# Two layers of recurrent mixing, routed experts and attention on one Trainium2 core: the choice of tokens moved into the layer 0 mixer and expert block

## The chip, the cores and the metric

The kernel runs on one core of one Trainium2 chip. The metric is the device time of one execution in microseconds. Three runs of the kernel before gave 1783.84, 1784.66 and 1787.1 us, so the median is 1784.66 us. TensorE does the matrix products and transposes, VectorE and ScalarE the elementwise work, GpSimd small elementwise work and indirect DMAs, and SyncE only issues DMAs.

## The reference, cut to what matters

Eight sequences of 512 tokens with 256 features each pass through two layers. This change touches layer 0 only. Its mixer and its experts both read the normalised input `xn`:

```python
qkv = rms_norm(xn) @ w_qkv.T;  q, k, v = split(qkv);  q, k = rms_norm(q), rms_norm(k)
w = exp(k);  y = sigmoid(q) * cumsum(w * v) / (cumsum(w) + 1e-6)      # along the sequence
u, g = split(y @ w_swiglu.T);  s = xn + (u * silu(g)) @ w_out.T       # the mixer

probs = softmax over the 512 tokens of (silu(xn @ router_w1) @ router_w2).T   # 16 experts a sequence
weights, tokens = top_k(probs, 64);  weights /= weights.sum() + 1e-9          # the choice of tokens
out_e = (silu(x_e @ w1[e]) * (x_e @ w2[e])) @ w3[e]                           # x_e: the chosen rows
f = scatter-add of weights * out_e;   x = x + s * silu(f)
```

Each of the 16 experts picks 64 of the 512 tokens of every sequence. So there are 8 x 16 = 128 lists, one for each partition. Layer 1 (attention with 16 heads, then 8 experts of which each token takes 2) follows and is not changed.

## The kernel before

The kernel is written engine by engine in blocks; all engines meet at the end of a block. Layer 0 has three of them.

`layer0_norm` normalises `xn`, keeps its transpose in `m.xnT`, and computes the router's logits. Its SyncE queue ends with eight 512 KB stores of zeros into `f`, the tensor to which the experts add (line 220).

`choose_tokens` (lines 108 to 184) is a block of its own. TensorE turns the logits so that each of the 128 partitions has one list of 512 (line 131). ScalarE takes the exponentials (L140). VectorE then runs eight rounds, each of which takes the eight largest values (L160), finds their places (L162) and strikes them out (L163). It scales the shares, adds the first row of the sequence to the places (L166 to L175), TensorE turns both tables back (L134, L135), and VectorE copies them to `k.slot_row` and `k.slot_share` (L182).

`layer0_mix_and_experts` does the rest. A product of the experts and of the mixer's gates is made of three products of `float32r` halves (`product3`, L93): each operand is split into a high part, copied by ScalarE, and a low part, subtracted by VectorE (`high_w` and `low_w` for the weights, `high_x` and `low_x` for the rows). The raw weights arrive in three tiles `raw[0..2]`. The swiglu weights of the mixer, `wsw`, come first and share `raw[0]` with `w1`.

Two lists set the order of every engine's work. `expert` has six entries for each expert: four `up` (a quarter of the hidden features each, both products) and two `down`. `mixing` has twelve for each sequence: four `qkv` (products of a tile of 128 tokens), four `sum` (the running sums, by products with a triangle and with ones; VectorE divides, L694 to L703), one `turn` (transposes of `y`), two `gates` and one `out`. `order` is made once and each engine walks through it: the first four `qkv`, then four `up` of expert 0, and from there one entry of `expert` and one of `mixing` by turns:

```python
order, LEAD = mixing[:T] + expert[:FC], FC
for i in range(len(expert) - LEAD):
    order += [expert[LEAD + i]] + mixing[T + i:T + i + 1]
order += mixing[T + len(expert) - LEAD:]
```

Some steps hang on others. `exps(n)` on ScalarE (exponentials of keys and of queries of sequence n) and `partial(n)` on GpSimd (sums of tiles, L634, L636) and `keys_values(n)` on VectorE (L686) come with the first `down` of expert 2n. `factors(n)` on GpSimd (L613 to L627) needs the squares of all four `qkv` of sequence n. `fetch(e)` on GpSimd gathers the 512 rows of expert e with four indirect DMAs (L644), `combine(e)` adds its results to `f` (L651), and the block ends when the last of these has landed. VectorE's queue begins with the low parts of `wsw`, `w1`, `w2` and `w3` (L746, L728), then comes the first copy of a qkv tile (L678, L679).

## Time and profile before

| | us |
|---|---|
| median of three runs | 1784.66 (1783.84 to 1787.1) |
| the profiled execution, its own time | 1782.32 |
| its span, first to last instruction | 1780.6 |
| the block that chooses tokens, TensorE's first to VectorE's last instruction | 51.12 to 74.37 |
| first product of the mixer | 75.06 |
| first product of expert 0 | 107.81 |
| last product of expert 15 | 617 |
| first load of layer 1 issued | 631.86 |

Over the whole span TensorE is busy 1573.8 us (88%), VectorE 1171.3 us (66%), ScalarE 922.1 us (52%) and GpSimd 729.9 us (41%). Such shares are means over stages with different limits, and the rows further down show the stage that the change touches. Times in the profile count from the first instruction. TensorE's granted clock is given as a share of its full speed, 1.00 being 2.4 GHz and 0.50 being 1.2 GHz. A matrix record overlaps the next one a little, so a busy time can exceed the time that passes.

### The profile page before, as it was taken

Reading aid. Unit: us, or ns where it says so; the run is one execution under the profiler, and the core shown is the slowest. Engines: PE = TensorE matmul, PEld = TensorE weight load, DVE = VectorE, ACT = ScalarE, POOL = GpSimd, SP = SyncE. Lnnn points to the kernel's source line nnn. Section 1 sums busy time; section 2 is a strip of 40 time slices with the busy share of each in tenths; the row PEclk is TensorE's granted clock in tenths of the full one; section 3 lists DMA queues with packets and bytes.
Section 4 is the critical chain, followed back from the end, with each engine's and each line's share of the span. In section 5 each row is a group of like instructions: output and inputs, shape, how many; then the busy total and the mean of one; then the engine's idle time right before and its main releaser. Section 6 shows DMA issues by size and latency. Waiting matters only on the chain.

```text
span 1780.6 us, 27053 instructions
## 1 busy us (share of the span) xinstructions
PE 1573.8 (88%) x9562; PEld 1141.8 (64%) x9562; DVE 1171.3 (66%) x1851; ACT 922.1 (52%) x1428; POOL 729.9 (41%) x661
## 2 busy tenths in 40 slices
PE   6269999999999829963899999999999999999975
PEld 4147787777777716641677777777777777777631
DVE  6536756756765536647666666777777777777647
ACT  2134554454454322310455556767776767676645
POOL 4213533443353254412233323455555555555410
PEclk9689999999999958985899999999999999999976
DMA  6423644644433167953334244666666666767464
GB/s 228 165 83 95 150 111 100 173 89 114 106 74 104 16 191 267 323 196 113 106 99 122 94 137 127 187 165 180 171 179 177 178 179 170 187 165 192 109 186 152
DMA packets 218919, 265.39 MB, mean 149 GB/s; under 512 B 19616, under 2 KB 160416, under 8 KB 218784
## 3 DMA queue, kind: packets, MB, share of 16 engines
q1 hardware_dynamic: 191904, 227.92, 42.2%
q0 software_dynamic: 26880, 35.73, 11.2%
q8 instruction: 77, 1.26, 0.3%
q14 instruction: 58, 0.48, 0.1%
HBM read 174.30 MB, written 88.75 MB: 148 GB/s over the span
## 4 chain that ended last, share of the span: by engine, by line
PE 38%; SPq 4%; DVE 4%; DMA 2%; ACT 1%; issue 1%; POOL 0%; DVEq 0%; ACTq 0%
PE a_hidden_bank L93 15%; PE a_bank L93 8%; PE a_bank L1519 5%; PE a_max_bank L1488 5%; PE a_score_bank L1509 3%; DMA a_ka<-qk 2%; SPq L1311 2%; SPq L1315 1%; PE a_max_bank L1534 1%; DVE a_neg_max L1784 1%; PE a_bank L1526 1%; DVE a_w20lo L1825 1%; ACT a_xThi L1667 1%; DVE a_hT1lo L1815 0%; SPq L1377 0%
## 5 line engine op out<-in xcount | busy, mean ns | idle before, releaser
L1645 ACT ACTIVATE a_prob<-a_score_bank 128x1024 f32<-128x1024 f32 x240 | 246.2, 1026 | 254.5 <-PE a_score_bank L1509 218.7
L1784 DVE TENSOR_REDUCE a_neg_max<-a_max_bank 128x2 f32<-128x1024 f32 x249 | 304.1, 1221 | 90.7 <-PE a_max_bank L1488 90.4
L1441 POOL DMA_INDIRECT fs<-a_y,a_token x80 | 127.1, 1589 | 188.9 <-ACT a_y L1693 165.1
L1488 PE MATMUL a_max_bank<-a_ka,a_qa 48*128 48x512 f32 x498 | 127.7, 509 | 23.2 <-DVE a_neg_max L1784 13.1
L1519 PE MATMUL a_bank<-a_prob,a_va 128*32 128x512 f32 x1024 | 145.8, 643 | 0.8 <-ACT a_prob L1645 0.6
L1807 DVE SCALAR_TENSOR_TENSOR a_tg<-a_tg,a_hidden_bank 128x512 f32<-128x512 f32 x112 | 76.8, 686 | 83.2 <-ACT a_tg L1655 83.2
L651 POOL DMA_INDIRECT f<-e_ye,c_slot_row x64 | 100.9, 1577 | 74.2 <-issue 50.5
L1509 PE MATMUL a_score_bank<-a_qa,a_ka 50*128 50x512 f32 x480 | 100.7, 415 | 5.4 <-DMA a_qa<-a_ml 3.0
L425 PE MATMUL e_bank<-m_wqkv,x_rows 128*128 128x512 f32 (+1 forms) x256 | 92.4, 506 | 14.7 <-DVE e_qkv L679 13.3
L739 DVE TENSOR_TENSOR e_h<-e_bank,e_sge 128x512 f32<-128x512 f32 x64 | 44.3, 692 | 85.8 <-ACT e_sge L563 85.3
L1488 PEld LDWEIGHTS a_max_bank<-a_ka,a_qa 48*128 48x128 f32 x498 | 47.9, 189 | 70.0 <-DVE a_neg_max L1784 27.6
L93 PE MATMUL a_hidden_bank<-a_xThi,a_w31hi 128*128 128x256 f32 x288 | 89.8, 312 | 0.0
L1655 ACT ACTIVATE a_tg<-a_hidden_bank 128x512 f32<-128x512 f32 x112 | 67.2, 600 | 41.9 <-PE a_hidden_bank L93 41.4
L644 POOL DMA_INDIRECT e_xg<-xn,c_slot_row x64 | 70.8, 1106 | 43.7 <-issue 43.7
L93 PE MATMUL e_bank<-e_w3hi,e_heThi 128*128 128x256 f32 x256 | 81.1, 317 | 7.8 <-DVE e_heTlo L743 7.8
L1811 DVE TENSOR_TENSOR a_h<-a_hidden_bank,a_tg 128x512 f32<-128x512 f32 x112 | 77.5, 692 | 13.0 <-PE a_hidden_bank L93 1.2
L93 PE MATMUL a_hidden_bank<-a_xThi,a_w11hi 128*128 128x256 f32 x288 | 85.0, 295 | 0.0
L93 PE MATMUL a_hidden_bank<-a_xThi,a_w31lo 128*128 128x256 f32 x288 | 82.5, 287 | 0.0
L93 PE MATMUL a_hidden_bank<-a_xTlo,a_w31hi 128*128 128x256 f32 x288 | 82.5, 286 | 0.0
L425 PEld LDWEIGHTS e_bank<-m_wqkv,x_rows 128*128 128x128 f32 x256 | 49.0, 197 | 52.1 <-issue 34.5
L93 PE MATMUL a_hidden_bank<-a_xTlo,a_w11hi 128*128 128x256 f32 x288 | 81.9, 284 | 0.0
L93 PE MATMUL a_hidden_bank<-a_xThi,a_w11lo 128*128 128x256 f32 x288 | 81.7, 284 | 0.0
(350 smaller groups left out, 4772.9 us busy)
## 6 DMA issues: line engine op xcount, KB each, us to landing
a_raw<-in_W SPq DMA_DIRECT2D x120, 512.0 KB, 4.9
e_raw<-in_w SPq DMA_DIRECT2D x48, 512.0 KB, 4.4
a_qa<-qk SPq DMA_DIRECT2D x192, 64.0 KB, 3.7
a_ka<-qk SPq DMA_DIRECT2D x192, 64.0 KB, 3.2
xs<-c_pad SPq DMA_DIRECT2D x20, 516.0 KB, 8.5
a_xg<-xs SPq DMA_DIRECT2D x20, 516.0 KB, 4.7
qk<-p_hi SPq DMA_DIRECT2D x32, 256.0 KB, 5.7
qk<-p_lo SPq DMA_DIRECT2D x32, 256.0 KB, 5.5
```

Source lines behind the costliest of these rows:

```text
L93: ins = nc.tensor.matmul(out, a[i][x], b[l][y], start=first and n == m == 0, stop=last and n == len(pairs) - 1 and m == 2)
L425: ins = nc.tensor.matmul(bank[:, 0:f1 - f0], m.xnT[:, n, ch, t * P:(t + 1) * P], m.wqkv[:, ch, f0:f1], start=ch == 0, stop=ch == DC - 1)
L644: nc.gpsimd.indirect_dma_start(xg[u][:, t, :], None, xn_rows, bass.IndirectOffsetOnAxis(k.slot_row[:, e, t:t + 1], 0)).then_inc(xg_in[u], 16)
L651: nc.gpsimd.indirect_dma_start(f_rows, bass.IndirectOffsetOnAxis(k.slot_row[:, e, t:t + 1], 0), ye[:, t, :], None, compute_op=ALU.add).the ...
L1441: nc.gpsimd.indirect_dma_start(f_rows, bass.IndirectOffsetOnAxis(token[x % 4][:, t:t + 1], 0), y[:, t, :], None, compute_op=ALU.add).then_ ...
L1488: nc.tensor.matmul(max_bank(g, m)[:, s, :], qa[q][rows, p, t * P:(t + 1) * P], ka[q][rows, p, :], start=True, stop=True).then_inc(p1_ps, 1)
L1509: nc.tensor.matmul(score_bank(g, u)[:, s, :], ka[q][rows, p, j * P:(j + 1) * P], qa[q][rows, p, :], start=True, stop=True).then_inc(s_ps, 1)
L1519: ins = nc.tensor.matmul(OB[rows, :], va[g % NR][:, j, rows], prob[j % 2][:, h_, :], start=j == 0, stop=j == T - 1, tile_position=(0, 32 * ...
L1645: nc.scalar.activation(prob[j % 2][:, 2 * p:2 * p + 2, :], score_bank(g, u)[:], ACT.Exp, scale=float(D) ** -0.5).then_inc(p_done, 1)
L1784: nc.vector.tensor_reduce(neg_max[:, g % 2, :, T * p + t], max_bank(g, m)[:], AX.X, ALU.max, negate=True).then_inc(mx_done, 1)
L1807: nc.vector.scalar_tensor_tensor(tg[:], tg[:], 1.0, GATE[:], ALU.add, ALU.mult).then_inc(act_done, 1)
L1811: nc.vector.tensor_tensor(h[:], VALUE[:], tg[:], ALU.mult).then_inc(h_done, 1)
```

## The change

The block `choose_tokens` is gone. Its steps stand at the beginning of `layer0_mix_and_experts`, before the walk through `order`, and its two score tiles and the tile of exponentials lie in `sge` and `h`, which the experts use later. The banks of `GATE` and `YE` hold its transposes.

- **VectorE** runs the eight rounds first, and after rounds 0, 2, 4 and 6 copies one qkv tile of sequence 0.
- **TensorE** turns the logits, does the four `qkv` of sequence 0 beside the rounds, turns the two tables, and then does four `sum` of sequence 0 and two `qkv` of sequence 1 before expert 0. The walk starts at `FIRST = 10` instead of 4 in `mixing`, so each sequence's steps lie beside the expert before, and the six entries of expert 15 have no mixer step after them.
- **GpSimd** makes the low parts of `wsw` and of the first weights in VectorE's place, then `factors(0)`, `fetch(0)`, `partial(0)` and `fetch(1)`.
- **ScalarE** alternates high parts with squares, and takes `exps(0)` before expert 0.
- **SyncE** loads `wsw` into `raw[2]` instead of `raw[0]`, so `w1` and `w2` need no wait and `w3` waits for the low part of `wsw`.

```diff
-def choose_tokens(nc, R, k):
...
+    prob, ex = [sge[:, i, :] for i in range(2)], h[:, 0, :]
...
+    LISTED, SLOTS = 2, 6
+    wsw_raw = raw[2][:].rearrange("p (c f) d -> p c (f d)", c=DC)
...
-    order, LEAD = mixing[:T] + expert[:FC], FC
+    FIRST = T + 6
+    order, LEAD = expert[:FC], FC
     for i in range(len(expert) - LEAD):
-        order += [expert[LEAD + i]] + mixing[T + i:T + i + 1]
-    order += mixing[T + len(expert) - LEAD:]
+        order += [expert[LEAD + i]] + mixing[FIRST + i:FIRST + i + 1]
...
-                elif i == 0:
-                    sp.wait_ge(yT_lo, 1)
+                elif i == 2:
+                    sp.wait_ge(wsw_lo, 1)
...
-            sp.dma_start(raw[0][:], wsw_d).then_inc(raw_in[0], 16)
-            for i in (1, 2, 0):
+            sp.dma_start(wsw_raw, wsw_d).then_inc(raw_in[2], 16)
+            for i in range(3):
                 load(i, 0)
...
+            for t in range(T):
+                ins = nc.tensor.transpose(GATE[:, t * P:(t + 1) * P], k.logits[:, t].rearrange("p b e -> p (b e)"), k.ident[:])
+            ins.then_inc(choice_ps, 1)
             pe.wait_ge(m.w_in, 2 * 16)
+            for t in range(T):
+                qkv_(0, t)
+            pe.wait_ge(choice_done, LISTED)
+            nc.tensor.transpose(YE[0][:, 0:P], rows[:].rearrange("p a c -> p (a c)"), k.ident[:])
+            nc.tensor.transpose(YE[1][:, 0:P], share[:].rearrange("p a c -> p (a c)"), k.ident[:]).then_inc(choice_ps, 1)
+            for t in range(T):
+                sum_(0, t)
+            qkv_(1, 0)
+            transpose_x(0)
+            qkv_(1, 1)
...
+            act.wait_ge(choice_done, 1)
+            nc.scalar.activation(ex, GATE[:], ACT.Exp, bias=neg_max[:], accum_out=total[:]).then_inc(choice_exp, 1)
+            act.wait_ge(raw_in[2], 16)
+            nc.scalar.activation(wsw[0][:], wsw_raw, ACT.Copy).then_inc(yT_hi, 1)
+            squared(0, 0)
             for i in range(3):
                 high_w(i, 0)
+                squared(0, i + 1)
+            exps(0)
+            squared(1, 0)
+            high_x(0)
+            squared(1, 1)
...
-                    if i == 0 and a % 2 == 0:
-                        exps(a // 2)
+                    if i == 0 and a % 2 and a + 1 < E0:
+                        exps((a + 1) // 2)
...
+            pool.wait_ge(yT_hi, 1)
+            nc.gpsimd.tensor_tensor(wsw[1][:], wsw_raw, wsw[0][:].bitcast(F32), ALU.subtract).then_inc(wsw_lo, 1)
+            for i in range(3):
+                low_w(i)
+            factors(0)
+            pool.wait_ge(choice_done, SLOTS)
             fetch(0)
+            partial(0)
             fetch(1)
...
-            dve.wait_ge(yT_hi, 1)
-            nc.vector.tensor_tensor(wsw[1][:], raw[0][:], wsw[0][:].bitcast(F32), ALU.subtract).then_inc(yT_lo, 1)
-            for i in range(3):
-                low_w(i, 0)
...
+            for r in range(CAP // 8):
+                eight, src, dst = best[:, 8 * r:8 * r + 8], prob[r % 2], prob[(r + 1) % 2]
+                own.step(nc.vector.max(eight, src))
+                own.wait()
+                own.step(nc.vector.max_index(place[:, 8 * r:8 * r + 8], eight, src))
+                own.step(nc.vector.match_replace(dst, eight, src, -1.0))
+                own.wait()
+                if r % 2 == 0:
+                    copy_qkv(0, r // 2)
...
+            keys_values(0)
+            for t in range(T):
+                divide(0, t)
+            copy_qkv(1, 0)
+            low_x(0)
+            copy_qkv(1, 1)
```

On VectorE, the end of the choice before the change and what stood behind it:

```order
L182 COPY c_slot_share<-ct_bank 64x64
L182 CAST c_slot_row<-ct_bank 64x64
L182 COPY c_slot_share<-ct_bank 64x64
L122 UNCONDITIONAL_BRANCH
L670 UNCONDITIONAL_BRANCH
L746 TENSOR_TENSOR e_wswlo<-e_raw,e_wswhi 128x1024
L728 TENSOR_TENSOR e_w10lo<-e_raw,e_w10hi 128x1024
L728 TENSOR_TENSOR e_w20lo<-e_raw,e_w20hi 128x1024
L728 TENSOR_TENSOR e_w3lo<-e_raw,e_w3hi 128x1024
L678 COPY e_qkv<-e_bank 128x512
L679 COPY e_qkv<-e_bank 128x256
```

The four low parts stand ahead of the first qkv copy here.

After the change the last two rounds read as follows, with the copy of the fourth qkv tile (L641 and L642 are the lines of L678 and L679) between them:

```order
L721 MAX e_best<-e_sge 128x8
L723 MAX_INDEX e_place<-e_best,e_sge 128x8
L724 MATCH_REPLACE e_sge<-e_best,e_sge 128x512
L641 COPY e_qkv<-e_bank 128x512
L642 COPY e_qkv<-e_bank 128x256
L721 MAX e_best<-e_sge 128x8
L723 MAX_INDEX e_place<-e_best,e_sge 128x8
L724 MATCH_REPLACE e_sge<-e_best,e_sge 128x512
```

The four subtractions of weights have left this queue, and the qkv copies now stand between the rounds.

On TensorE, the choice and the first tile's products before (the last row of the first fence is followed by three more such pairs, then by the transposes of the gathered rows):

```order
L131 MATMUL ct_bank<-c_ident,c_logits 128x128 x4
L134 MATMUL ct_bank<-c_ident,ct_rows 128x128
L135 MATMUL ct_bank<-c_ident,ct_share 128x128
L122 UNCONDITIONAL_BRANCH
L419 UNCONDITIONAL_BRANCH
L425 MATMUL e_bank<-m_wqkv,x_rows 128x512 x2
L425 MATMUL e_bank<-m_wqkv,x_rows 128x256 x2
```

All products of the mixer stand behind both tables' transposes here.

And the changed queue behind the fourth tile's products, from the two tables' transposes (L434, L435) to those of the gathered rows (L403) and the products behind them:

```order
L434 MATMUL e_bank<-c_ident,e_rows 128x128
L435 MATMUL e_bank<-c_ident,e_share 128x128
L369 MATMUL e_bank<-e_wkv,c_upper 128x512 x2
L372 MATMUL e_bank<-e_wkv,c_ones 128x512
L369 MATMUL e_bank<-e_wkv,c_upper 128x512
L372 MATMUL e_bank<-e_sums,c_ones 128x512
L369 MATMUL e_bank<-e_wkv,c_upper 128x512
L372 MATMUL e_bank<-e_sums,c_ones 128x512
L358 MATMUL e_bank<-m_wqkv,x_rows 128x512 x2
L358 MATMUL e_bank<-m_wqkv,x_rows 128x256 x2
L403 MATMUL e_bank<-c_ident,e_xg 128x128 x8
L358 MATMUL e_bank<-m_wqkv,x_rows 128x512 x2
```

The running sums (L369, L372) and the products of sequence 1 now lie ahead of the transposes of expert 0's rows.

On GpSimd the changed kernel's block begins with the four low parts, and the gathers of expert 0 stand behind the factors of sequence 0; before, the eight gathers came first:

```order
L611 TENSOR_TENSOR e_wswlo<-e_raw,e_wswhi 128x1024
L608 TENSOR_TENSOR e_w10lo<-e_raw,e_w10hi 128x1024
L608 TENSOR_TENSOR e_w20lo<-e_raw,e_w20hi 128x1024
L608 TENSOR_TENSOR e_w3lo<-e_raw,e_w3hi 128x1024
L564 TENSOR_SCALAR e_small<-e_ssq 128x8
L567 TENSOR_TENSOR e_small<-e_small,m_r2sq 128x4 x2
L571 TENSOR_SCALAR e_small<-e_small 128x8
L573 TENSOR_TENSOR e_small<-e_small,m_half 128x8
L577 TENSOR_TENSOR e_scale<-e_small,m_r2neg 128x4
L578 TENSOR_TENSOR e_scale<-e_small,m_r 128x4
L595 DMA e_xg<-xn,c_slot_row 128x256 x4
L585 TENSOR_TENSOR e_sums<-e_wkv 128x512
```

The gathers (L595) moved behind six small steps and four large ones, and the partial sums (L585, L587) moved between the two experts' gathers.

## Rows read from the trace of the kernel before

**Rows 1.** Windows: from:to, length, busy us (records) per engine, TensorE clock, DMA share, GB/s
```profile
50.00:55.00 5.00, 0.84 (x6) 0.53 (x6) 2.80 (x9) 2.06 (x3) 0.13 (x1) 0.88 1.00 333
...
133.00:587.40 454.40, 441.44 (x2147) 341.57 (x2146) 291.88 (x426) 229.67 (x455) 191.81 (x176) 1.00 0.45 109
...
587.40:617.00 29.60, 27.42 (x138) 21.53 (x137) 18.18 (x26) 9.92 (x16) 6.26 (x4) 1.00 0.17 18
```

**Rows 2.** Timeline, the block that chooses: start us, duration, engine, line, operation, tiles
```profile
51.12 0.63 PE L131 MATMUL ct_bank<-c_ident,c_logits 128*128 128x128 f32 x4 [0.90 <-PEq L200]
...
54.04 0.69 DVE L160 MAX8 ct_best<-ct_prob 128x8 f32<-128x512 f32 x1
...
71.47 0.22 DVE L166 TENSOR_REDUCE ct_wsum<-ct_best 128x1 f32<-128x64 f32 x1
...
74.15 0.22 DVE L182 COPY c_slot_share<-ct_bank 64x64 f32<-64x64 f32 x1
```

**Rows 3.** Timeline, opening of the mixer and expert block
```profile
75.06 5.46 PE L425 MATMUL e_bank<-m_wqkv,x_rows 128*128 128x512 f32 x8 [1.47 <-PEq L122]
...
79.06 1.06 ACT L580 ACTIVATE e_wswhi<-e_raw 128x1024 fp32r<-128x1024 f32 x1 [25.78 <-DMA e_raw<-in_w_swiglu]
...
85.86 1.06 ACT L552 ACTIVATE e_w10hi<-e_raw 128x1024 fp32r<-128x1024 f32 x1 [5.74 <-DMA e_raw<-in_w]
...
90.47 0.69 DVE L678 COPY e_qkv<-e_bank 128x512 f32<-128x512 f32 x1
...
91.08 0.41 DVE L679 COPY e_qkv<-e_bank 128x256 f32<-128x256 f32 x1
```

**Rows 4.** Timeline, from the last opening copy to the first expert product, and GpSimd's factors
```profile
105.00 0.42 ACT L522 ACTIVATE e_squares<-e_qkv 128x256 f32<-128x256 f32 x1 [3.06 <-DVE e_qkv L679]
...
106.09 0.24 POOL L613 TENSOR_SCALAR e_small<-e_ssq 128x8 f32<-128x8 f32 x1 [20.14 <-issue]
...
106.42 1.29 DVE L733 TENSOR_TENSOR e_xeTlo<-e_bank,e_xeThi 128x512 fp32r<-128x512 f32 x2 [1.45 <-ACT e_xeThi L558]
...
107.81 0.47 PE L93 MATMUL e_bank<-e_xeThi,e_w10hi 128*128 128x512 f32 x1 [3.03 <-issue]
...
109.21 0.20 POOL L627 TENSOR_TENSOR e_scale<-e_small,m_r 128x4 f32<-128x4 f32 x1
```

**Rows 5.** TensorE alone, expert 0, whose up products have no mixer step between them
```profile
113.80 0.50 PE L93 MATMUL e_bank<-e_xeThi,e_w10hi 128*128 128x512 f32 x1 [1.41 <-DVE e_h L739]
...
118.27 0.50 PE L93 MATMUL e_bank<-e_xeThi,e_w10hi 128*128 128x512 f32 x1 [1.41 <-DVE e_h L739]
...
128.87 0.58 PE L93 MATMUL e_bank<-e_w3hi,e_heThi 128*128 128x256 f32 x1 [2.08 <-DVE e_heTlo L743]
...
132.24 1.08 PE L469 MATMUL e_bank<-c_ident,e_xg 128*128 128x128 f32 x8
```

**Rows 6.** GpSimd: one of eight gathers (timeline), and the second partial sum (line's rows)
```profile
85.00 0.95 POOL L644 DMA_INDIRECT e_xg<-xn,c_slot_row  x1 [0.30 <-issue]
...
L636 POOL TENSOR_TENSOR e_sums<-e_sums,e_wkv x8: 1266/1295/1297, 132.9 to 583.1; 128x512 f32<-128x512 f32 x8
```

**Rows 7.** VectorE timeline, first and last instruction of one division of a tile
```profile
588.08 0.42 DVE L694 SCALAR_TENSOR_TENSOR e_den<-e_bank,e_qkv 128x256 f32<-128x256 f32 x1 [0.56 <-PE e_bank L439]
...
590.79 0.42 DVE L703 TENSOR_TENSOR e_y<-e_bank,e_den 128x256 f32<-128x256 f32 x1
```

**Rows 8.** TensorE timeline: pieces of a sum, a qkv step, an output step
```profile
141.35 1.02 PE L436 MATMUL e_bank<-e_wkv,c_upper 128*128 128x512 f32 x2
...
142.21 1.02 PE L439 MATMUL e_bank<-e_sums,c_ones 128*128 128x512 f32 x2
...
150.99 2.74 PE L425 MATMUL e_bank<-m_wqkv,x_rows 128*128 128x512 f32 x8
...
617.03 3.62 PE L460 MATMUL e_bank<-m_wout,e_guT 128*128 128x256 f32 x16
```

**Rows 9.** GpSimd's product of two SBUF tiles in layer 1 (tile's rows: ns min/median/max)
```profile
L971 POOL TENSOR_TENSOR p_xas<-p_xa,p_lnw_row x32: 718/726/1703, 648.2 to 762.4; 128x256 f32<-128x256 f32 x32
```

132 lines of the change are left out of this document (48 added, 84 removed).

## The prediction

> **What bounds the kernel now.** I read the windows by stage first, then the timeline from the end of the normalisation to the first expert, then the end of expert 15. From 133 us to 587.4 us TensorE is busy 441.4 of 454.4 us at clock 1.00 [rows 1], so what leaves or enters there counts in TensorE time alone. Before that stretch nothing fills it. The choice is a chain on VectorE: TensorE turns the logits at 51.12, the rounds start at 54.04 and end at 71.47 (8 rounds, 2.18 us each), and the last table is copied at 74.37 [rows 2]. Then the mixer's first qkv step runs at 1.2 GHz (5.46 us), its result is ready at 80.5, but VectorE copies it only at 90.47 [rows 3]. The reader sees why in the two ScalarE rows: they wait for the transfers of the raw weights, and VectorE's low parts stand in its queue ahead of the copy. The first expert product starts at 107.81, 2.8 us after the squares that follow the last qkv copy [rows 4]. So 56.7 us pass from the logits to expert 0 with TensorE mostly idle, and two causes follow each other that don't need each other: the rounds, and the weights with the qkv steps.
>
> **The opening after the change.** The rounds still start at 54.04: the block before ends as it did, and the tables of the logits need nothing new. Four copies of qkv tiles go between them, 1.02 us from the start of one to its end [rows 3], 1.05 with the step to the next. They need TensorE's result each time: a qkv step at full clock is 2.74 us [rows 8], the next copy comes 4.4 us later, so VectorE doesn't wait. The rounds end at 71.5 + 4.2 = 75.7. The tail of the choice is 2.9 us as before [rows 2]: the tables are there at 78.6.
>
> Beside it, off this chain: the zeros stored into `f` hold all DMA engines until about 55 (333 GB/s, share 1.00) [rows 1]; the swiglu weights, 512 KB, then need some 1.6 us, so about 57, and their high part 1.06 [rows 3], 58.1. GpSimd's low parts have no row. The nearest is its partial sum, 1.29 us for 512 columns [rows 6], so 2.6 us for 1024; the upper bound is below. By this they end near 60.7 and 63.3, the third waits for ScalarE, which alternates high parts with squares of copies, and ends near 68, and the fourth near 73. SyncE's load of `w3` waits for the first low part (60.7) and lands well before 70; behind it in that queue are only zeros. I cost all this at nothing, the cover being the rounds. The squares of the fourth tile, copied at 73.5, are ready at 74.4; `factors(0)` takes 109.41 - 106.09 = 3.3 us [rows 4], to 77.7, one microsecond ahead of the tables. That microsecond is all the slack this cover has.
>
> Then the chain on VectorE: four products of keys and values, priced like one pass of a division at 0.42 [rows 7], to 80.3. Four divisions of 591.21 - 588.08 = 3.13 us each [rows 7]. The third needs GpSimd's first partial sum: four gathers at 1.25 us a piece (0.95 and 0.30 between) [rows 6] from 78.7 to 83.7, the sum to 85.0, the products of the running sum 1.72 (two pairs of 0.86) [rows 8] to 86.7, just when two divisions end (86.6). The divisions end at 92.9, the copy of the first tile of sequence 1 at 93.9, and squares and split of the gathered rows take the same 2.8 us as before [rows 4]: 96.8. TensorE's second qkv step of that sequence fits beside (93.9 + 2.74). I take **97.0 for the first expert product instead of 107.81: -10.8 us**. The bounds: 95 if GpSimd and VectorE lose nothing between steps, and 104 by the rival below.
>
> The first `up` took 5.99 us (107.81 to 113.80), the second 4.47 (to 118.27) [rows 4, 5], for it ran at 1.2 GHz after 3 us without work. Now a qkv step ends just before it, but a table load on ScalarE comes later than before relative to it. Between nothing and -1.5 I take **-1.0**.
>
> **The walk.** Four `sum` and two `qkv` of TensorE leave it: 0.86 + 3 x 1.72 + 2 x 2.74 = 11.5 us [rows 8]. Up to expert 15 the same number of slots is filled, so the six last mixer steps now lie before it: two sums 3.4, a turn 0.9 (like the 8 transposes of 1.08 with overlap [rows 5]), two gates of twelve products, each about as long as an `up` without its idle time (4.47 - 1.41, less 0.3 of the last one's end, is 2.75 [rows 5]), and an output 3.6 [rows 8], 13.4 us in all. TensorE being the bound, **+1.9**.
>
> **Expert 15** took 29.6 us with its mixer steps [rows 1]. Alone it looks like expert 0: from its second `up` (113.80) to the end of its first `down` (132.24) 18.4 us [rows 5], a first `up` of 4.5, and a second `down` of 24 products. Fifteen of them took 3.37 us at 1.2 GHz (128.87 to 132.24) [rows 5], so 24 at full clock take 2.7. That makes 25.6: **-4.0**. What follows (combining, landing of the last addition, the next block) keeps its length, and the mixer's output is no longer beside it.
>
> **Sum:** -10.8 - 1.0 + 1.9 - 4.0 = -13.9. The profiled execution took 1782.32 us, so it would be 1768.4; the median of the runs is 2.3 above it, so I forecast 1784.66 - 13.9, rounded, **1771 us**.
>
> **Two rules weighed.** GpSimd's product of two SBUF tiles took 726 ns in the median and 1703 ns at worst [rows 9]; the eight rounds each read one SBUF tile, and no row shows GpSimd beside them. The Trainium skill, SBUF — State Buffer, section "SBUF: two separate sides", says that the two engines exclude each other on a shared port pair only while a VectorE instruction has two SBUF inputs or runs in a two-port mode; by that the rounds and copies would collide with nothing, and the sum stays as it is. If the worst row held all along, it is the first rival.
> TensorE idled 2.08 us before 128.87 and resumed at 1.2 GHz, but kept 4.47 us periods after idle times of 1.41 us [rows 5]. The Trainium skill, TensorE: Matmul & The Clock Gate, section "HAM oscillation — how this bites in real kernels", describes bursts between waits that start slow every time. That speaks against spacing qkv steps between rounds and against leaving expert 15 unfilled; the sum would be the last rival's.
>
> **Rivals.**
> *GpSimd becomes the bound of the opening (0.15).* Its subtractions contend with VectorE and take 1703/726 of 2.6, 6.1 us each: from 58.1 to 82.5, `factors(0)` at 85.8 instead of 77.7, the first expert product 7 us later, at 104. For it: the slack is one microsecond, and rows 9. Against: the rounds read one tile. -13.9 + 7 = -6.9, 1778 us.
> *The walk gives some back (0.10).* Its 13 us of idle time [rows 1] hang on which step lies beside which; each sequence's steps now lie beside experts of the other parity. Half as much again is +6: -7.9, 1777 us. Against: SyncE's, GpSimd's and ScalarE's steps are shifted with them.
> *More is gained (0.10).* The clock stays at 1.00 into both `down` of expert 15 (1.6 less) and the opening ends at 95 with all of the 1.5 on the first `up`: -18, 1766.5 us.
> *Slower: TensorE stays at 1.2 GHz through the opening and through expert 15 (0.05).* Then a qkv step is 5.46 [rows 3] against 4.4 between copies (+3.3 over three), the last one of the opening costs 2.7 more, four `up` of expert 0 cost about 2.5 more each (twelve products at twice 0.23), and in expert 15 four `up` another 10 and the `down` 4: +30 in all, 1801 us. It decides from the point at which more than 17.5 of these 30 are paid. For it: the spaced steps, and the half clock at 75.06 [rows 3]. Against: expert 0's periods of 4.47 at full clock with the same idle times [rows 5].
>
> **Chances.** The forecast has 0.60, with its own range 1767 to 1775. A measurement of this kernel can tell about 0.2% (3.6 us) from no change. All cases but the last are faster by more than that, except for the far ends of the first two rivals together: faster 0.92, same 0.03, slower 0.05. The range from 1765 to 1779 leaves out the slow rival, a part of the best case, and the ends of the first two.
>
> **What would show it.** Right: VectorE's rounds end near 75.7 and the tables at 78.6; GpSimd's low parts take about 2.6 us and `factors(0)` ends before 78.6; the first expert product stands near 97; from the first `up` of expert 1 to that of expert 15 TensorE is as busy as before and the stretch about 2 us longer; expert 15 takes some 25.6 us. Wrong: low parts of 5 us or more, key and value products that wait for ScalarE's exponentials, an expert 0 that starts after 102, an `up` in expert 15 with a period over 5 us, or a walk with more than 3% idle time.

## The result, and the profile after

The changed kernel takes **1769.73 us** (median of 5 runs, 1767.77 to 1774.72). The kernel before takes 1784.37 us (5 runs, 1780.07 to 1787.1). The ratio is 0.9922, with a 95% interval from 0.9905 to 0.9939. The forecast was 1771. The profiled execution took 1770.29 us, with a span of 1768.3 us and a mean granted clock of 0.942. Before, that was 1782.32 us, 1780.6 us and 0.938.

The windows by stage of the changed kernel (from:to, length, then busy us and number of records of TensorE, its weight loads, VectorE, ScalarE and GpSimd, the granted clock, DMA share, GB/s) answer to [rows 1]:

```profile
51.00:75.00 24.00, 15.14 (x36) 7.56 (x36) 20.98 (x51) 9.32 (x23) 9.37 (x4) 0.86 0.67 218
75.00:99.00 24.00, 15.80 (x40) 7.39 (x40) 19.22 (x38) 5.33 (x16) 13.56 (x17) 0.79 0.44 129
99.00:580.30 481.30, 461.32 (x2253) 359.53 (x2251) 298.62 (x435) 238.92 (x465) 191.96 (x176) 1.00 0.43 104
580.30:604.00 23.70, 17.73 (x97) 14.45 (x96) 7.87 (x11) 6.71 (x11) 4.76 (x4) 1.00 0.20 22
```

The walk is as full as before: 461.3 busy of 481.3 us (96%) at clock 1.00, and before, from the first product of expert 0 on, 460.3 of 479.6. It begins at 99 instead of 107.8. In the 48 us ahead of it VectorE is busy for 40.2 us, in both windows more than any other engine, and TensorE's clock is 0.86 and 0.79. Expert 15 now takes 23.7 us instead of 29.6, and its clock is 1.00 although TensorE is busy only 75% of it.

The timeline of the rounds (start, duration, engine, line, operation, tiles; in brackets the idle time before it and what ended it) answers to [rows 2, 3]:

```profile
54.72 0.69 DVE L721 MAX8 e_best<-e_sge 128x8 f32<-128x512 f32 x1
...
59.35 2.36 POOL L611 TENSOR_TENSOR e_wswlo<-e_raw,e_wswhi 128x1024 fp32r<-128x1024 f32 x1 [13.21 <-ACT e_wswhi L527]
...
68.54 4.54 PE L358 MATMUL e_bank<-m_wqkv,x_rows 128*128 128x512 f32 x8 [2.44 <-DVE e_qkv L642]
...
73.19 0.69 DVE L641 COPY e_qkv<-e_bank 128x512 f32<-128x512 f32 x1 [0.48 <-PE e_bank L358]
...
76.30 0.22 DVE L728 TENSOR_REDUCE e_wsum<-e_best 128x1 f32<-128x64 f32 x1
...
78.44 0.20 POOL L578 TENSOR_TENSOR e_scale<-e_small,m_r 128x4 f32<-128x4 f32 x1
...
79.12 0.22 DVE L746 COPY c_slot_share<-e_bank 64x64 f32<-64x64 f32 x1
```

The rounds with their four copies last from 54.72 to 76.30, 21.6 us: eight times 2.18 and four copies of 0.94, and one wait of 0.48 for the fourth qkv step, which took 4.54 us and not 2.74. GpSimd's low parts take 2.35 us, and its factors are ready at 78.64, 0.7 us before the tables (79.34).

From the tables to the first two `up` of expert 0, same view (answers to [rows 4, 5, 7]):

```profile
79.91 3.78 PE L369 MATMUL e_bank<-e_wkv,c_upper 128*128 128x512 f32 x4 [1.35 <-DVE e_wkv L649]
80.27 1.48 POOL L595 DMA_INDIRECT e_xg<-xn,c_slot_row  x1 [1.63 <-DVE c_slot_share L746]
...
82.02 0.42 DVE L657 SCALAR_TENSOR_TENSOR e_den<-e_bank,e_qkv 128x256 f32<-128x256 f32 x1 [0.98 <-PE e_bank L369]
...
85.49 0.42 DVE L657 SCALAR_TENSOR_TENSOR e_den<-e_bank,e_qkv 128x256 f32<-128x256 f32 x1 [0.34 <-PE e_bank L372]
...
86.98 1.10 PE L369 MATMUL e_bank<-e_wkv,c_upper 128*128 128x512 f32 x2 [1.58 <-POOL e_sums L585]
...
89.03 0.42 DVE L657 SCALAR_TENSOR_TENSOR e_den<-e_bank,e_qkv 128x256 f32<-128x256 f32 x1 [0.41 <-PE e_bank L372]
...
94.90 0.42 DVE L666 TENSOR_TENSOR e_y<-e_bank,e_den 128x256 f32<-128x256 f32 x1
...
97.32 1.06 ACT L503 ACTIVATE e_xeThi<-e_bank 128x512 fp32r<-128x512 f32 x2
...
99.32 0.47 PE L93 MATMUL e_bank<-e_xeThi,e_w10hi 128*128 128x512 f32 x1
...
104.07 0.50 PE L93 MATMUL e_bank<-e_xeThi,e_w10hi 128*128 128x512 f32 x1 [1.76 <-DVE e_h L702]
```

The running sums come late for VectorE three times (0.98, 0.34, 0.41 us). The first two waits go with the clock: the four products from 79.91 took 3.78 us, where at full clock a pair takes 1.02 to 1.10. The third does not: the pair at 86.98 ran at full clock (1.10 us) but had waited for GpSimd's first partial sum, which ended at 86.83 behind four gathers issued from 80.27 to 85.54. The four divisions end at 95.32. The copy and the split of the gathered rows follow, and the first expert product starts at 99.32. The second `up` starts 4.75 us after it.

TensorE's timeline at both places, the first `down` of expert 0 and that of expert 15:

```profile
119.13 0.39 PE L93 MATMUL e_bank<-e_w3hi,e_heThi 128*128 128x256 f32 x1 [2.08 <-DVE e_heTlo L706]
...
120.33 0.42 PE L93 MATMUL e_bank<-e_w3hi,e_heTlo 128*128 128x256 f32 x1
...
599.45 0.39 PE L93 MATMUL e_bank<-e_w3hi,e_heThi 128*128 128x256 f32 x1 [1.73 <-DVE e_heTlo L706]
...
604.11 0.28 PE L93 MATMUL e_bank<-e_w3hi,e_heTlo 128*128 128x256 f32 x1
```

After its wait of 2.08 us TensorE starts at full clock (0.28 us a record behind the first) in expert 0 and falls to 1.2 GHz (0.42) after six records; in expert 15 it does not fall in this run. Fifteen such products took 2.7 us from 119.13 and 2.0 from 599.45, against 3.37 in [rows 5].

Where the 12.3 us between the two spans came from, each start taken from the two timelines:

| piece | before | after | difference | forecast |
|---|---|---|---|---|
| start to first expert product | 107.81 | 99.32 | -8.5 | -10.8 |
| first `up` of expert 0 | 5.99 | 4.75 | -1.2 | -1.0 |
| second `up` of expert 0 to first `up` of expert 15 | 473.62 | 476.16 | +2.5 | +1.9 |
| first `up` of expert 15 to its last product | 29.49 | 23.88 | -5.6 | -4.0 |
| last product to layer 1's first load | 14.95 | 15.01 | +0.1 | 0 |
| layer 1 | 1148.7 | 1149.2 | +0.5 | 0 |

### The profile page after: what moved, and what is told of

Same layout as the page of the kernel before. It is cut to its first block, busy times and chain, and to the rows that moved or that the text cites. A ratio compares the mean times of both kernels' runs of the same rounds, so it can differ in the third digit from the quotient of the medians.

```text
span 1768.3 us, 27041 instructions
## 1 busy us (share of the span) xinstructions
PE 1576.7 (89%) x9562; PEld 1140.3 (64%) x9562; DVE 1166.1 (66%) x1847; ACT 918.9 (52%) x1426; POOL 739.4 (42%) x664
## 4 chain that ended last, share of the span: by engine, by line
PE 39%; SPq 4%; DVE 3%; DMA 2%; ACT 1%; issue 1%; POOL 0%; DVEq 0%; ACTq 0%
PE a_hidden_bank L93 16%; PE a_bank L93 8%; PE a_bank L1522 5%; PE a_max_bank L1491 5%; PE a_score_bank L1512 3%; DMA a_ka<-qk 2%; SPq L1314 2%; SPq L1318 2%; PE a_max_bank L1537 1%; PE a_bank L1529 1%; DVE a_w20lo L1828 1%; ACT a_xThi L1670 1%; DVE a_neg_max L1787 1%; DVE a_hT1lo L1818 0%; SPq L1380 0%
## 5 line engine op out<-in xcount | busy, mean ns | idle before, releaser
L1787 DVE TENSOR_REDUCE a_neg_max<-a_max_bank 128x2 f32<-128x1024 f32 x249 | 304.1, 1221 | 91.8 <-PE a_max_bank L1491 86.2
L508 ACT ACTIVATE e_sge<-e_bank 128x512 f32<-128x512 f32 x64 | 38.1, 595 | 81.1 <-PE e_bank L93 81.1
L595 POOL DMA_INDIRECT e_xg<-xn,c_slot_row x64 | 70.9, 1108 | 20.7 <-issue 18.6
```

Of the source, the lines that this page charges most:

```text
L595: nc.gpsimd.indirect_dma_start(xg[u][:, t, :], None, xn_rows, bass.IndirectOffsetOnAxis(k.slot_row[:, e, t:t + 1], 0)).then_inc(xg_in[u], 16)
L1787: nc.vector.tensor_reduce(neg_max[:, g % 2, :, T * p + t], max_bank(g, m)[:], AX.X, ALU.max, negate=True).then_inc(mx_done, 1)
```

## The experiments

The experiments form three series. Each has the kernel before in it (medians 1783.08, 1783.37 and 1783.01), and each ratio is to the kernel before of its own series. The series of 1783.37 ran on another chip than the other two; it holds the low parts on VectorE, the three more subtractions, the restored phase and the first run with unread products.

**The change again.** No edit; it is the yardstick for the runs beside it.

> The changed kernel once more, on the same chip and beside the same runs of the kernel before as the three variants. Both theories: about 1769 to 1770 us, 0.992 of before; first expert product at 99.3 us, first product of expert 15 at 580.2, last one at 604.4.

Measured: 1768.82 us (6 runs, 1767.91 to 1770.34), ratio 0.9923 [0.9902, 0.9944]. The first round started at 55.16 and the first expert product at 99.60, within 0.5 us of the trace above. Starts agree to about that between profiles of one kernel. Layer 1, which no edit touches, took 1146.4 us here and 1149.2 above: 3 us between two profiles can come from there.

**The choice in its own block again**, with its steps on each engine taken out of the mixer and expert block, all else of the change kept.

```diff
+            with ExitStack() as ctx:
+                choose_tokens(nc, Room(nc, ctx, "ct_"), k)
             with ExitStack() as ctx:
                 layer0_mix_and_experts(
...
+            for t in range(T):
+                copy_qkv(0, t)
```

> Everything of the change but one: the choice of tokens has its own block again, and the new opening (qkv of sequence 0, low parts on GpSimd, four sums and two qkv steps ahead of expert 0) starts when it is over. Theory A (the gain is the rounds lying beside the loads, splits and qkv steps): the opening's chain starts at about 75 instead of 51.5. Fourth qkv copy near 96, factors near 100, keys and values 102, four divisions to 114.5, first expert product near 118 instead of 99.3 and 107.8 before. With the walk 2 us longer and expert 15 5.6 us shorter than before this is slower than before by about 6 us, 1790 us. Theory B (the gain comes from the six mixer steps taken ahead and the bare expert 15, the rounds' place matters little): it keeps most of the gain, 1770 to 1775 us.

Measured: 1790.21 us (8 runs), 1.0040 [1.0020, 1.0060], slower than the kernel before. VectorE's timeline of the first and the last of the four copies, and TensorE's first expert product:

```profile
80.61 0.69 DVE L704 COPY e_qkv<-e_bank 128x512 f32<-128x512 f32 x1 [5.56 <-PE e_bank L430]
...
92.50 0.69 DVE L704 COPY e_qkv<-e_bank 128x512 f32<-128x512 f32 x1 [2.94 <-PE e_bank L430]
...
117.90 0.47 PE L93 MATMUL e_bank<-e_xeThi,e_w10hi 128*128 128x512 f32 x1
```

Each of the last three copies waits 2.94 us for a qkv step of TensorE, so the four qkv steps and all behind them are a chain of their own behind the rounds. The first expert product stands at 117.90, 18.6 us after that of the change. Without the overlap nothing of the opening's gain is left: the four `sum` and two `qkv` before expert 0 then only lengthen it, 10.1 us against the kernel before, while expert 15 gives 4.1 back (25.4 us instead of 29.5; it took 23.9 in the change, more on this below). The whole gain at the front is the rounds beside other work.

**The four copies behind the rounds.**

```diff
-                if r % 2 == 0:
-                    copy_qkv(0, r // 2)
+            for t in range(T):
+                copy_qkv(0, t)
             own.step(nc.vector.tensor_reduce(wsum[:], best[:], AX.X, ALU.add))
```

> The changed kernel with the four qkv copies behind the eight rounds instead of between them. Theory A (the copies must stand between the rounds because each qkv step of TensorE waits for the copy before it): the rounds end 4.7 us earlier, but then come a copy and three times a qkv step and a copy in line, 3.95 us each at full clock and up to 6.6 at 1.2 GHz; the fourth copy ends 8 to 13 us later than now, the squares, high parts and GpSimd's low parts that alternate with them too, and the first expert product stands at 107 to 113; 1777 to 1782 us. Theory S (only that the rounds lie beside the weights' loads counts): within 2 us of the changed kernel.

Measured: 1781.71 us (10 runs), 0.9981 [0.9966, 0.9996]. The timeline:

```profile
72.68 4.99 PE L358 MATMUL e_bank<-m_wqkv,x_rows 128*128 128x512 f32 x8 [18.22 <-DVE e_qkv L642]
...
90.88 0.20 POOL L578 TENSOR_TENSOR e_scale<-e_small,m_r 128x4 f32<-128x4 f32 x1
...
111.26 0.47 PE L93 MATMUL e_bank<-e_xeThi,e_w10hi 128*128 128x512 f32 x1
...
612.93 0.41 PE L93 MATMUL e_bank<-e_w3hi,e_heTlo 128*128 128x256 f32 x1
```

TensorE stood idle for 18.2 us before the second qkv step, which waits for the first tile's copy. GpSimd's later low parts and its factors follow the copies (90.88 instead of 78.44). The first expert product moves by 12 us, and the run loses most of the change's gain: 12.9 us by the medians, about 10 by the ratios. It is not enough that both chains lie in one block: the copies have to stand between the rounds in VectorE's queue, since TensorE, ScalarE and GpSimd each need the copy before they go on.

The last row shows something else. Expert 15 is bare here as in the change, with the same periods of its `up`, but inside its first `down` the clock falls (0.41 us a record instead of 0.28), and it lasts 25.4 us instead of 23.9. Eight of the fourteen profiles have a bare expert 15. It took 23.88 us in four of them (the change in both its profiles, three more subtractions, the changed kernel with unread products) and 25.35 to 25.37 in the other four (the own block, this run, the low parts on VectorE, expert 0's rows first).

**The low parts on VectorE** as before the change, but one behind each odd round.

```diff
-            pool.wait_ge(yT_hi, 1)
-            nc.gpsimd.tensor_tensor(wsw[1][:], wsw_raw, ...).then_inc(wsw_lo, 1)
-            for i in range(3):
-                low_w(i)
...
+                elif r == 1:
+                    dve.wait_ge(yT_hi, 1)
+                    nc.vector.tensor_tensor(wsw[1][:], wsw_raw, ...).then_inc(wsw_lo, 1)
+                else:
+                    low_w((r - 3) // 2, 0)
```

> The changed kernel with the four low parts back on VectorE, one after each odd round, so GpSimd does nothing before the factors. Theory A (VectorE's queue is the opening's chain, and every instruction taken off it shortens the opening): four times 1.22 us plus steps, less the 0.5 us that the fourth copy waited for TensorE: the tables stand at about 83.8 instead of 79.3, the first expert product at about 104, the time 4 to 5 us over the changed kernel, 1773.5 us. Theory B (it did not matter which engine subtracts, the chain waits for something else): no difference, 1769 us.

Measured: 1776.18 us (4 runs), 0.9956 [0.9940, 0.9973]. From its timeline:

```profile
68.33 1.23 DVE L682 TENSOR_TENSOR e_w10lo<-e_raw,e_w10hi 128x1024 fp32r<-128x1024 f32 x1
...
81.17 1.23 DVE L682 TENSOR_TENSOR e_w3lo<-e_raw,e_w3hi 128x1024 fp32r<-128x1024 f32 x1
```

The subtraction takes 1.23 us on VectorE against 2.35 on GpSimd, and still the run is longer: from its first round (56.62) to the first expert product (105.32) 48.7 us pass instead of 44.6. The rounds with copies and low parts take 25.7 us instead of 21.6: 4.1 more, four times 1.15 (a low part's step), less the wait of 0.48 for the fourth qkv step, which is gone. VectorE is the chain, and GpSimd's slower copy of the work costs nothing. The run is 2.7 us above what I expected. Layer 1 starts 7.9 us later than in the change: 4.1 of that is the subtractions, 1.9 lies ahead of the first round (56.62 instead of 54.72), before any edited step, 1.5 is a fall of the clock in expert 15, and the rest lies in the walk.

**Three more subtractions on GpSimd** before the last low part, 128 x 1024 each. They write tiles that nobody has filled or reads yet, so the output is the same.

```diff
+                if i == 2:
+                    for spare in (yT[1], guT, xeT[1]):
+                        nc.gpsimd.tensor_tensor(spare, raw[i][:], dst[0][:].bitcast(F32), ALU.subtract)
                 nc.gpsimd.tensor_tensor(dst[1][:], raw[i][:], dst[0][:].bitcast(F32), ALU.subtract)
```

> The changed kernel with three more subtractions of 128x1024 on GpSimd, into tiles that hold nothing yet, before the low part of w3. Theory A (GpSimd had slack in front of the factors, 2.5 us by its wait for the squares in the changed kernel's trace, and then under a microsecond more): the three take 7.05 us, so the factors end near 83.2 instead of 78.6, keys and values start 4 us later, the gathers 3 us later, and the first expert product stands near 103.5; 1773 us. The rounds keep their 2.18 us. Theory C (GpSimd and VectorE slow each other, the first rival of the prediction): GpSimd's instructions or the rounds beside them get longer than 2.36 and 2.18 us, and the loss is 7 us or more.

Measured: 1772.99 us (4 runs), 0.9941 [0.9922, 0.9960]. From its timeline:

```profile
70.25 2.35 POOL L610 TENSOR_TENSOR e_yTlo<-e_raw,e_w3hi 128x1024 fp32r<-128x1024 f32 x1 [2.94 <-ACT e_w3hi L497]
...
77.16 2.36 POOL L611 TENSOR_TENSOR e_w3lo<-e_raw,e_w3hi 128x1024 fp32r<-128x1024 f32 x1
...
82.57 0.20 POOL L578 TENSOR_TENSOR e_scale<-e_small,m_r 128x4 f32<-128x4 f32 x1
...
83.45 1.67 DVE L652 SCALAR_TENSOR_TENSOR e_wkv<-e_qkv,m_r,e_wkv 128x256 f32<-128x256 f32 x4 [1.87 <-ACT e_wkv L475]
```

The three take 6.9 us; the factors end at 82.77 instead of 78.64 (+4.1), the rest having been slack of GpSimd in front of the last low part. VectorE now waits 1.87 us for ScalarE's exponentials. Counted from the first round, the factors are 4.3 us later and the first product 3.9 (48.5 instead of 44.6), so the slack behind the factors was only some 0.4 us, less than the 0.7 between them and the tables, since ScalarE's exponentials stand in between. All seven subtractions of GpSimd beside the rounds took 2.35 to 2.37 us each, and a round still took 2.18. So the first rival's price did not exist here, but its threshold did: the change lies within 1 us of the point from which GpSimd sets the opening.

**None of the six steps ahead.** The four `sum` and two `qkv` of the mixer go back into the walk, beside expert 1.

```diff
-    FIRST = T + 6
+    FIRST = T
...
-            for t in range(T):
-                sum_(0, t)
-            qkv_(1, 0)
             transpose_x(0)
-            qkv_(1, 1)
...
-            keys_values(0)
-            for t in range(T):
-                divide(0, t)
-            copy_qkv(1, 0)
             low_x(0)
-            copy_qkv(1, 1)
```

> The choice inside the block and beside the first qkv steps and weights, as in the change, but none of the six mixer steps goes ahead: the walk starts at the first sum, as before, and expert 15 has its mixer steps again. Theory A: the tables are there at 79.3, the last gather is issued near 85 and lands 4.5 us later, so the first expert product stands near 93 (6 us before the changed kernel's). The walk and expert 15 take what they took before (479.6 and 29.7 us). So about 14 us under before, 1770 us, the same as the changed kernel within 2 us: the six steps ahead gave nothing. Theory B: without the six steps ahead most of the gain is gone, 1778 us or more.

Measured: 1765.27 us (6 runs), 0.9895 [0.9873, 0.9917], against 0.9923 [0.9902, 0.9944] of the change in the same series, and 5 us below what I expected, which was no gain over the change. The intervals overlap, but the slowest of the six runs (1765.55) is faster than the fastest of the change beside it (1767.91), and in the profiles layer 1 starts at 614.91 instead of 619.20. The timeline:

```profile
86.17 1.97 PE L403 MATMUL e_bank<-c_ident,e_xg 128*128 128x128 f32 x8 [8.56 <-DMA e_xg<-xn,c_slot_row]
...
90.19 0.77 PE L93 MATMUL e_bank<-e_xeThi,e_w10hi 128*128 128x512 f32 x1 [2.06 <-issue]
...
90.75 0.63 PE L93 MATMUL e_bank<-e_xeTlo,e_w10hi 128*128 128x512 f32 x1
...
97.06 0.49 PE L93 MATMUL e_bank<-e_xeThi,e_w10hi 128*128 128x512 f32 x1 [1.41 <-DVE e_h L694]
```

Now the gathered rows pace: they are there at 86.2, and the first expert product starts at 90.19, 9.1 us before that of the change. More than half of it is paid back. The first `up` runs at 1.2 GHz throughout (records of 0.63 us behind the first) and lasts 6.9 us, and expert 15 has its mixer steps again (29.5 us instead of 23.9). In the change the fourth gather is issued 1.2 us later than here, so the rows must be there near 87.4 (an estimate from the two issue times), but their transposes stand at 93.09 and their split at 97.32, behind VectorE's divisions.

**Expert 0's rows first, part of the six behind.** Three `sum` stay ahead, the fourth and the two `qkv` stand between the `up` of expert 0.

```diff
-    order, LEAD = expert[:FC], FC
+    LEAD = FC
+    order = [expert[0], mixing[T + 3], expert[1], mixing[T + 4], expert[2], mixing[T + 5], expert[3]]
...
-            for t in range(T):
-                sum_(0, t)
-            qkv_(1, 0)
+            sum_(0, 0)
+            sum_(0, 1)
             transpose_x(0)
-            qkv_(1, 1)
+            sum_(0, 2)
```

> The changed kernel, its walk from down 0 of expert 0 on unchanged (six steps ahead, expert 15 bare), but the six steps no longer all stand before expert 0: two sums and two divisions, then the gathered rows' transposes and split, then the third sum and division; the fourth sum and the two qkv steps of sequence 1 lie between expert 0's up products. Theory A (in the changed kernel the gathered rows have landed by 87 and their split waits until 97 behind four divisions, a copy and squares): the first expert product stands near 91 instead of 99.3, expert 0's up products have periods near 5.2 instead of 4.45, the walk behind starts 6 us earlier; 1763 us, level with the variant that was restored to the walk's old pairing (1761.4 us). Theory R (the six steps ahead cost in the walk or the bare expert 15, not in the opening): no earlier start of down 0, 1769 us.

Measured: 1765.35 us (5 runs), 0.9891 [0.9867, 0.9915], the same as with none ahead. The first product stands at 90.81 and the second `up` 4.44 us behind it, at full clock, but the third and fourth `up` follow 5.3 us apart, because a qkv step of sequence 1 now stands before each. Layer 1 starts at 614.64; 1.5 us of the 2.4 by which the run misses the forecast of 1763 is the fall of the clock in expert 15 (25.4 us). The steps ahead of expert 0 gain nothing by themselves; they only must not stand in front of the rows.

**The sums between expert 0's `up`, in another phase.** This run was to beat the change. The opening is that with none of the six ahead, but `exps(0)`, `keys_values(0)` and `partial(0)` stay in it; the walk starts with the first entries of both lists.

```diff
-    FIRST = T + 6
-    order, LEAD = expert[:FC], FC
+    FIRST = T
+    order, LEAD = [], 0
```

> As the variant with none ahead, but the walk begins with expert 0's first up product, so its four up products have the four sums of sequence 0 between them, and only the last four entries of expert 15 are bare. Exponentials, keys and values of sequence 0 stay in the opening. Theory A: first expert product near 93, the sums fill idle time of TensorE of 1.4 us each in expert 0, expert 15 takes 27 to 28 us: about 3 us under the changed kernel, 1766 to 1767 us. Theory B: with no step ahead it is no better than the kernel before by more than 5 us, 1778 us or more.

Measured: 1792.68 us (7 runs), 1.0059 [1.0038, 1.0080]: some 26 us above what I expected. The first expert product did stand early (91.21). The loss is in the walk: from expert to expert it takes 34.7 and 33.0 us in turn, 67.7 for two, where the kernel before and the change take 30.5 and 33.5, 64.1. Over seven pairs that is 25 us. The walk's waits of TensorE between 130 and 550 us, first of the change, then of this run (engine, tile, line, who was waited for: us in total, times, longest):

```profile
PE e_bank L93 <- DVE e_h L702: 5.8, 12, 0.5
PE e_bank L93 <- DVE e_heTlo L706: 5.0, 6, 0.8
```

```profile
PE e_bank L93 <- DVE e_h L696: 17.7, 25, 1.0
PE e_bank L93 <- DVE e_heTlo L700: 8.6, 6, 1.4
```

`e_h` is late 25 times instead of 12, and 17.7 us in total instead of 5.8. In all TensorE idles for 27.9 of these 420 us instead of 11.2. All of mixing[4:] lies four entries earlier against the experts' entries here, so other mixer steps fall beside `up` and `down` than before. The change shifts them by six, which is one whole expert (four `up`, two `down`), so the same kinds meet again: 5.8 and 5.0 us of waits against 6.1 and 5.7 before.

**The same with the phase restored.** Only expert 0's four `up` get the four sums; its `down` and the first two `up` of expert 1 go bare, so that from there on each step stands where it stood before. With the steps go `exps`, `partial` and `keys_values` of the later sequences, from the first `down` of odd experts back to that of even ones (not shown).

```diff
-    order, LEAD = [], 0
+    order = [entry for t in range(T) for entry in (expert[t], mixing[T + t])] + expert[T:2 * T]
+    for i in range(2 * T, len(expert)):
+        order += [expert[i], mixing[i]]
```

> As the variant that begins the walk with expert 0's up products and puts the four sums of sequence 0 between them, which took 1792.7 us, but the entries down 0, down 1, up 0 and up 1 after these are bare, so that from there on every mixer step lies beside the same expert entry as in the kernel before. Theory P (that variant lost its time because its walk puts all four sums of a sequence beside up entries and gates or outputs beside down entries, 67.6 us for two experts instead of 64.0): the walk is back at 64.0 us for two experts and the time is 1763 to 1765 us, at or a little below the variant with no step ahead (1765.3 us). Theory Q (the loss came from filling expert 0's up products, or from the opening with the exponentials ahead): it stays near 1790 us.

Measured: 1761.35 us (4 runs), 0.9880 [0.9864, 0.9897]. From expert 2 on the experts take 30.5 to 31.2 and 33.5 to 33.7 us again, and layer 1 starts at 611.64. So the phase of the walk was the cause, and not the filled `up` or the opening: with the same opening work, four entries of shift cost some 28 us of layer 0 (639.40 to 611.64). Which pairing does the harm, and whether the three helpers that move with the steps have a part in it, these two runs don't tell apart; the change has the helpers beside odd experts too and loses nothing.

**TensorE kept busy in the changed kernel's opening.** Products of the mixer's weights that nobody reads, behind each qkv step.

```diff
                 qkv_(0, t)
+                for _ in range(2 if t < 3 else 4):
+                    nc.tensor.matmul(MIX[1][:], k.upper[:], m.wqkv[:, 0, 0:2 * D], start=True, stop=True)
```

> The changed kernel with TensorE kept busy in the opening by ten products of 128x512 whose result nobody reads: two after each of the first three qkv steps of sequence 0 and four after the fourth. Theory A (the lower clock cost the opening what the trace shows: 1.2 GHz in the fourth qkv step and in the first sums, with VectorE waiting 0.5, 1.0 and 0.3 us for them): the clock stays at 1.00, the first expert product stands 1.5 to 2 us earlier, near 97.5, the time near 1767 us, at the edge of what can be told. Theory B (VectorE's divisions set the pace anyway): no difference in the first expert product beyond 0.5 us.

Measured: 1765.89 us (4 runs), 0.9896 [0.9880, 0.9913]. The first expert product stands at 99.96 and the start of layer 1 at 619.60, not earlier than in the change. The products did hold the clock up through the rounds: the fourth qkv step takes 2.85 us instead of 4.54. But TensorE idles for 2.6 us before the tables, and the sums are slow again:

```profile
68.67 2.85 PE L358 MATMUL e_bank<-m_wqkv,x_rows 128*128 128x512 f32 x8 [0.72 <-DVE e_qkv L644]
...
77.56 0.33 PE L436 MATMUL e_bank<-c_ident,e_rows 128*128 128x128 f32 x1 [2.61 <-DVE e_rows L741]
...
79.55 3.60 PE L369 MATMUL e_bank<-e_wkv,c_upper 128*128 128x512 f32 x4 [1.55 <-DVE e_wkv L651]
...
87.66 1.91 PE L372 MATMUL e_bank<-e_sums,c_ones 128*128 128x512 f32 x2
...
89.67 0.42 DVE L659 SCALAR_TENSOR_TENSOR e_den<-e_bank,e_qkv 128x256 f32<-128x256 f32 x1 [1.89 <-PE e_bank L372]
```

This is not the case that Theory B describes. The fourth copy no longer waits (0.48 us won), and the sum ahead of the second division is in time. But the low clock now falls on the sum ahead of the third (1.91 us for the pair at 87.66, 1.02 in the change), and VectorE waits 1.89 us for it instead of 0.41. From the first round to the first expert product 45.1 us pass instead of 44.6. So these products moved the low clock and did not remove it, and TensorE's speed did count; what the opening takes with all sums at full clock no run shows. The median is 3 us below the change's of another series, and nothing in the opening, the walk or expert 15 accounts for that. I count it as not told apart.

**The same products, with nine more that fill the wait for the gathered rows, on the kernel with none ahead.**

```diff
+            for _ in range(9):
+                nc.tensor.matmul(MIX[1][:], k.upper[:], m.wqkv[:, 0, 0:2 * D], start=True, stop=True)
             transpose_x(0)
```

> The variant with no step ahead (1765.3 us) with products that nobody reads between its qkv steps and, nine of them, while it waits for the gathered rows. In that variant expert 0's first up product ran at 1.2 GHz and took 6.9 us instead of 4.45. If the idle wait is what lowers the clock, the transposes of the rows and the first up product now run at 2.4 GHz: 2.5 to 3.5 us less, 1762 us. If the idle time isn't the cause, or TensorE's speed doesn't count there: first up product still 6.9 us, or no difference in the time.

Measured: 1757.96 us (4 runs), 0.9861 [0.9837, 0.9885], against 0.9895 [0.9873, 0.9917] without them. Its timeline:

```profile
77.42 9.59 PE L439 MATMUL e_bank<-m_wqkv,c_upper 128*128 128x512 f32 x18
...
86.84 1.04 PE L403 MATMUL e_bank<-c_ident,e_xg 128*128 128x128 f32 x8
...
89.93 0.47 PE L93 MATMUL e_bank<-e_xeThi,e_w10hi 128*128 128x512 f32 x1 [2.06 <-issue]
...
94.33 0.50 PE L93 MATMUL e_bank<-e_xeThi,e_w10hi 128*128 128x512 f32 x1 [1.41 <-DVE e_h L698]
```

The transposes take 1.04 us instead of 1.97, all records of the first `up` are at full clock, and it lasts 4.40 us instead of 6.87. Layer 1 starts at 610.55 instead of 614.91: 4.4 us, 2.5 of them in the first `up`, 0.3 in the first product's start, 1.7 in the two `down` of expert 0, where the clock no longer falls, none in expert 15. The medians, of two series, differ by 7.3 and the profiled executions by 12.1. In the profiled ones what exceeds 4.4 lies in layer 1, whose instructions are the same: 1140.6 us here, against 1145.1 to 1149.2 in all kernels but the two with the nine products. I have no row that ties this to the products.

**And on the restored phase**, the same nine products.

> The variant with the sums of sequence 0 in expert 0's up products and the old pairing behind it (1761.4 us) with the same unread products. Its first up product took 5.7 us and the transposes of the rows ran at 1.2 GHz; at full clock 2 us less, 1759 to 1760 us, the fastest of all. If TensorE's clock there doesn't count: 1761 us again.

Measured: **1756.46 us** (5 runs), 0.9846 [0.9826, 0.9867], the lowest median of all, by the ratios 0.8% below the change. Here the nine products don't hold the clock: it falls inside the first `up`, although TensorE had been at work up to the transposes 2.1 us ahead of it.

```profile
89.70 0.47 PE L93 MATMUL e_bank<-e_xeThi,e_w10hi 128*128 128x512 f32 x1 [2.06 <-issue]
...
90.24 0.52 PE L93 MATMUL e_bank<-e_xeThi,e_w10lo 128*128 128x512 f32 x1
...
90.55 0.63 PE L93 MATMUL e_bank<-e_xeThi,e_w10hi 128*128 128x512 f32 x1
...
95.69 0.50 PE L93 MATMUL e_bank<-e_xeThi,e_w10hi 128*128 128x512 f32 x1 [0.55 <-DVE e_h L699]
```

The first `up` takes 6.0 us, no less than without the products (5.7), and layer 1 starts at 610.76, only 0.9 earlier, which the faster transposes give. The forecast time came out (even lower), the reason given for it did not. The other 6.4 us between the profiled executions lie in layer 1 (1138.7 us, 1145.1 without). The medians differ by 4.9, from two chips. That the same nine products held the clock in the last run and not in this one says that one profile is not enough for what they are worth. The two filled kernels can't be told apart from each other.

## Why the prediction was right

**What bounds the kernel: right.** The two causes were independent, and one beside the other is worth what the shorter one takes. With the choice apart the changed kernel loses to the kernel before (0.4%), and with the copies behind the rounds it keeps 0.2%.

**The rounds with four copies: right.** 21.6 us forecast (54.04 to 75.7), 21.6 measured. A copy with the step to the next cost 0.94 and not 1.05; the difference was eaten by a wait of 0.48 for the fourth qkv step.

**GpSimd's low parts at no cost: right, and tight.** 2.35 us instead of 2.6, and 0.7 us between factors and tables instead of one, of which some 0.4 was slack. The extra subtractions confirm both the hiding and its end. The rule that the first rival was weighed against (the Trainium skill, SBUF — State Buffer, section "SBUF: two separate sides") agrees with what the runs show here: a round with one SBUF input took 2.18 us beside GpSimd's subtraction as it did alone, and the subtraction 2.35 us as in the own block, where no round runs beside it (2.34 to 2.35). That GpSimd's product in [rows 9] ranges up to 1703 ns was no sign for this place.

**The first expert product: mechanism right, size off by 2.3 us.** Forecast 97.0, measured 99.32. The term that failed is "four divisions of 3.13 us each", taken as if TensorE's sums were always ahead. A division did take that, but VectorE waited 0.98, 0.34 and 0.41 us for sums. The first two waits go with the low clock (3.78 us for four products). The third is another term of the forecast, the partial sum ready at 85.0: the gathers ahead of it began at 80.27 and not at 78.7, and it ended at 86.83. The other 0.7 us is the start of the first round, 54.72 instead of 54.04; over all profiles it lies between 53.9 and 56.6 us. Copies and splits behind the divisions took what they took before.

**The first `up`: right**, -1.2 for -1.0. **The walk: right**, +2.5 for +1.9, but not where I looked for it. The stretch from the first `up` of expert 1 to that of expert 15, which I said would be about 2 us longer, took 448.9 us against 449.2. The excess lies behind the two `down` of expert 0, where two qkv steps stand now (2.74 each) and two sums stood before (0.86 and 1.72). The waits of the walk's rows didn't grow. The second rival (the walk gives some back) is a real mechanism, at a larger price than I gave it: a shift that is no whole expert cost 25 us. It did not occur since six steps are one expert. I had not counted that as a reason against the rival, and should have.

**Expert 15: mechanism right, size off by 1.6 us in this run.** Forecast 25.6, measured 23.9 and clock 1.00. The term "18.4 us from its second `up` to the end of its first `down`" carried over from expert 0 the fifteen products at 1.2 GHz (3.37 us); here they took 2.0. In the four other kernels with a bare expert 15 in which the clock fell, it took 25.4, close to the forecast; so the 1.6 us came and went with the clock, and I can't say from these runs what decides it. It is what the third rival said of expert 15, without its opening at 95. The slower rival is refuted: periods of 4.44 us and clock 1.00 with a busy share of 75%. The Trainium skill (TensorE: Matmul & The Clock Gate, "HAM oscillation — how this bites in real kernels") describes bursts that start slow every time. The change agrees in part: in the opening the clock was 0.79 to 0.86, but the second and third qkv steps, after idle times of 1.56 and 2.44 us, took 2.85 us each, which is full clock, and only the fourth took 4.54; in expert 15 every burst started at full clock.

**Sum.** -13.9 forecast; the traces give -12.7 to the start of layer 1, where +2.3 (sums and start) and -1.6 (expert 15) partly cancel, +0.6 the walk; and -14.6 between the medians. That the median comes within 1.3 us of the forecast is in part luck: two misses of opposite sign, and medians 2.3 us further apart than the two profiled spans.

What I did not see: four `sum` and two `qkv` ahead of expert 0 were the weak part of the change. I costed them as the chain to the first product, without asking whether the rows of expert 0 needed them. They don't. With none of them ahead layer 1 starts 4.3 us earlier, and with the sums in the idle time between expert 0's `up` 7.5 us earlier (611.64 against 619.12).

## What to carry to other kernels

When two chains that don't need each other follow one another on one engine, put the steps of one between those of the other in that engine's queue, and look at the slack of each engine that gets the displaced work: here it was under 0.7 us. When steps of one list are shifted against another list that they are interleaved with, shift by a whole period of it, or look at which kinds meet: four entries cost 25 us, six cost nothing. Before a stretch of products that is short and waits for others, see whether the clock there is low because of idle time before it, and whether TensorE's speed is on the chain there. Then see in the trace whether filling the idle time does hold the clock: it gave 4.4 us up to layer 1 where it held, 0.9 where the same products did not hold it, and nothing where the low clock only moved to a later sum.
